# A four-layer decoder kernel: VectorE takes the layer-norm statistics ahead of two additions, and TensorE's first scores wait for the raw maxima

## The reference

```python
x = x + attention(layernorm(x))           # 16 heads of 8 channels
x = x + cross_attention(layernorm(x), ctx)
x = x + feed_forward(layernorm(x))        # experts, BitLinear, experts, attention with experts
```

## Time and profile before

| what | value |
|---|---|
| median of three runs | 4897.14 us |
| the profiled execution | 4900.09 us |
| its span | 4898.2 us |
| mean granted TensorE clock | 0.889 of full speed |
| busy: TensorE, its weight loads | 4007.7 us (82%), 2918.6 us (60%) |
| busy: VectorE, ScalarE, POOL | 3203.4 us (65%), 2059.5 us (42%), 2994.6 us (61%) |

### The profile page before, as it was taken

One profiled execution on the slowest core, in us unless ns is written; L12 is line 12 of the kernel. 1 busy time (PEld: TensorE's weight loads), 2 busy tenths in 40 slices (PEclk: granted clock), 3 DMA queues, 4 the chain that ended last, 5 costly groups with the idle time before them and its releaser, 6 DMA issues. The chain is left out here.

```text
span 4898.2 us, 215645 instructions
## 1 busy us (share of the span) xinstructions
PE 4007.7 (82%) x85067; PEld 2918.6 (60%) x85076; DVE 3203.4 (65%) x10848; ACT 2059.5 (42%) x5737; POOL 2994.6 (61%) x4949
## 2 busy tenths in 40 slices
PE   8999977254899978656999997559879998889988
PEld 6777754132566666523777774335547776667766
DVE  5875668422344688787556874753337878888866
ACT  4555545011344444365555554112225543336632
POOL 6766632276455699688556762038876777777710
PEclk9999988555899998755999997879998999999999
DMA  3000012433100022200000002113431000000000
GB/s 94 5 13 19 19 28 57 78 62 54 37 0 0 18 39 39 35 1 1 2 0 15 22 18 54 42 46 75 77 62 35 0 15 16 16 9 1 0 13 24
DMA packets 380509, 139.58 MB, mean 28 GB/s; under 512 B 216487, under 2 KB 373239, under 8 KB 380055
## 3 DMA queue, kind: packets, MB, share of 16 engines
q1 hardware_dynamic: 345430, 107.60, 9.3%
q0 software_dynamic: 34816, 28.34, 4.0%
HBM read 91.46 MB, written 43.85 MB: 28 GB/s over the span
## 5 line engine op out<-in xcount | busy, mean ns | idle before, releaser
L1051 DVE TENSOR_REDUCE rowmax<-ps 128x16 f32<-128x1024 f32 x512 | 626.3, 1223 | 488.0 <-PE ps L678 487.7
L696 PE MATMUL ps<-prob,kT 32*64 32x256 f32 x9216 | 781.7, 408 | 8.7 <-issue 2.4
L721 PE MATMUL ps<-v,probT 64*64 64x64 f32 x36864 | 764.6, 227 | 5.3 <-issue 2.2
L721 PEld LDWEIGHTS ps<-v,probT 64*64 64x64 f32 x36864 | 683.8, 140 | 57.4 <-issue 16.0
L678 PE MATMUL ps<-kblock,qT 32*64 32x256 f32 x8192 | 697.0, 410 | 17.2 <-DVE rowmax L1060 14.2
L900 ACT ACTIVATE probT<-ps 128x1024 f32<-128x1024 f32 x512 | 518.0, 1012 | 353.4 <-PE ps L708 353.0
L585 POOL TENSOR_TENSOR kblock<-kT,key_scale 128x512 f32<-128x512 f32 x576 | 599.8, 1041 | 18.2 <-ACT kT L878 7.6
L587 POOL TENSOR_TENSOR prob<-qT,key_scale 128x512 f32<-128x512 f32 x576 | 601.5, 1044 | 0.0
L561 POOL TENSOR_TENSOR vareps<-moments,eps 128x1 f32<-128x1 f32 x522 | 98.8, 189 | 745.7 <-DVE negmean L1025 745.6
L887 ACT ACTIVATE xn<-x_res,nmr,rstd 128x128 f32 (+1 forms) x512 | 252.7, 494 | 513.6 <-POOL nmr L567 349.5
L708 PEld LDWEIGHTS ps<-mT,pick_bf 32*64 32x64 bf16 x16384 | 311.7, 108 | 221.2 <-ACT mT L857 74.1
(11 more groups left out here) (380 smaller groups left out, 9655.7 us busy)
## 6 DMA issues: line engine op xcount, KB each, us to landing
ctxT<-in_ctxT SPq DMA_DIRECT2D x256, 64.0 KB, 1.8
held<-in_g_w SPq DMA_DIRECT2D x16, 836.0 KB
ctxT<-in_ctxT SPq DMA_DIRECT2D x256, 32.0 KB, 1.9
table<-prob SPq DMA_DIRECT2D x32, 256.0 KB, 2.4
x_dram<-x_res SPq DMA_DIRECT2D x32, 256.0 KB, 2.4
x_res<-x_dram SPq DMA_DIRECT2D x16, 512.0 KB, 6.9
x_res<-in_x SPq DMA_DIRECT2D x8, 512.0 KB, 7.5
x_res<-in_e_w SPq DMA_DIRECT2D x64, 64.0 KB
```

The lines of the kernel that those rows point to most:

```text
L696: mm = nc.tensor.matmul(out.rearrange("p (h s) -> p h s", h=GH), k.kT[rows, buf, S * b:S * b + S], k.qblock[rows, buf, :, S * b:S * b + S] ...
L721: mm = nc.tensor.matmul(k.ps_o[S * b:S * b + S, u, S * hh:S * hh + S], k.probT[rows, buf, at:at + S], k.v9[rows, buf, (HD + 1) * h:(HD + 1 ...
L1051: nc.vector.tensor_reduce(spread, heads, AX.X, ALU.max).then_inc(soft.did["max_raw"], 1)
```

## The change

In `scores_writable` TensorE waits for `max_raw` (L1051 has read the bank `s1`) in place of `max_done` (L1060 is through). In VectorE's step the output addition and the value bias move from ahead of the incoming tile's statistics to behind them. The four statistics instructions, their waits and the two additions are the same as before.

```diff
     def scores_writable(score1, score2, it):
         if score1 is not None:
-            after(pe, c, "max_done", it, 4)
+            after(pe, c, "max_raw", it, 4)
             after(pe, c, "kblock_done", it, 3)
...
             post_sums(post, pb, it, par)
-        if out is not None:
-            xt = stream_of(k, out.name)[:, out.columns()]
-            after(dve, c, "bias_done", it, 8)
-            dve.wait_ge(c.yv_psum, it - 2)
-            nc.vector.tensor_tensor(xt, xt, k.ps_y, ALU.add).then_inc(out.did["y_read"], 1)
-        if value is not None and value.name in VALUE_BIAS:
...
         early = c.prenormed(it, -PRENORM)
...
         if start is not None and not both:
...
             nc.vector.tensor_scalar(k.negmean[:, par, 0:1], k.meanvar[:, par, 0:1], -1.0, None,
                                     ALU.mult).then_inc(start.did["mv_done"], 1)
+        if out is not None:
+            xt = stream_of(k, out.name)[:, out.columns()]
+            after(dve, c, "bias_done", it, 8)
+            dve.wait_ge(c.yv_psum, it - 2)
+            nc.vector.tensor_tensor(xt, xt, k.ps_y, ALU.add).then_inc(out.did["y_read"], 1)
+        if value is not None and value.name in VALUE_BIAS:
...
         if guard is not None:
```

More of the change, by code:

```diff
@@ L1026, in step @@
                                     ALU.mult).then_inc(start.did["mv_done"], 1)
+        if out is not None:
[4 more added lines that the diff above has]
+        if value is not None and value.name in VALUE_BIAS:
+            bias = k.bv[:, value.a, :]
+            dve.wait_ge(c.yv_psum, it - 2)
+            if value.name == "L1_xattn":
+                after(dve, c, "v_done", it, 3 + NB)
+                nc.vector.tensor_tensor(k.v_sum[:, b3, :], k.ps_v, bias, ALU.add).then_inc(value.did["v_raw"], 1)
+            else:
+                after(dve, c, "o_psum", it, 3 + NB)
+                nc.vector.tensor_tensor(values(k, b3), heads_of(k.ps_v), heads_of(bias),
+                                        ALU.add).then_inc(value.did["v_done"], 1)
         if guard is not None:
```

## The result

The changed kernel takes **4981.45 us** (median of six runs, 4976.48 to 4994.65) against 4896.65 us before (six runs, 4893.37 to 4898.26): a ratio of 1.0177 with the 95% interval 1.0164 to 1.019, 85 us slower. The forecast was 4968, with 4912 to 4992 as its range. The total was right; two of its parts were not, and they cancelled.

What follows compares the result with a forecast made beforehand. Unmasked attention stages were taken as a ring of two arms meeting at POOL's kblock, masked ones as held by TensorE. Order +71 us, wait 0: 4900.1 + 71 = 4971, less 3 to the median, 4968 us; range 4912 to 4992.

Steps and rivals of the forecast that it cites:

- the longer arm: L0_attn, L2_xattn, L3_attn, L3_ffn: statistics arrive last at kblock, kT has 0.39 to 0.64 us slack; the move makes kT last.
- 0.53 behind L1019, plus 0.15 - 0.08 = 0.07, in all 0.60 us later: L0_attn: output addition L992 starts behind L1025, so oT and all later ScalarE instructions, kT included, come 0.60 us later.
- I take 0.09 us from ScalarE's or VectorE's end to the next engine's start: Handover between engines, read from L992's end to oT's start and also used from kT's end to POOL's kblock: 0.09 us.
- 0.30: L0_attn: later kT delays kblock, +0.30 us a step; the like terms were +0.19 in L2_xattn and +0.23 in L3_attn.
- +0.49 + 0.20 = +0.69: L3_ffn, us a step: kblock 0.49 later for kT, plus 0.20 because L1057 falls into L587 and L1060 follows.
- L3_xattn, -0.22: The one stage where the move pays: statistics no longer behind L1001, which stood 0.22 ahead of L1019; -0.22 us a step.
- The cover of L1001's own delay: L3_xattn: TensorE is idle before it needs oT, so L1001's delay costs nothing; without this cover up to 0.60 us.
- The masked stages' cover: L0_xattn, L1_attn, L2_attn: TensorE sets the step and needs the later kT and mT only later; costed at 0.
- Rival (c): Masked stages lose their cover and L585's delay counts in 180 steps: +34 to +54 us, 5002 to 5022; chance 0.08.
- I take 0, being nearest to the row that is not released by L1060: Masked stages, new wait ahead of L794: gain between 0 and 0.25 us a step, taken as 0.
- rival (a): The masked wait was real: L794 comes up to 0.25 us earlier, -45 us, total 4923; chance 0.18.
- the forecast's 1.19 a step: Sum of the order's terms over five stages, 0.30 + 0.19 + 0.23 + 0.69 - 0.22; times 60 steps, +71 us.

Runs made afterwards that it cites:

- e4: Changed kernel with ScalarE evicting qT and kT ahead of mT and xnT, TensorE waiting for mT and xnT by themselves: 4935.90 us.
- e9: Kernel before with max_raw wait, statistics first in L3_xattn, additions mid-statistics in L0_attn, L2_xattn, L3_attn and between L3_ffn's two sets: 4854.68 us.
- e5: Changed kernel with the waits of the two additions, not the additions, put ahead of the statistics: 4980.09 us.
- e6: Changed kernel with POOL waiting for s2_psum ahead of kT_done instead of behind it: 4977.42 us.
- e2: Kernel before with only VectorE's order changed, TensorE still waiting for max_done: 5033.61 us, ratio 1.0288.
- e1: Kernel before with only TensorE's wait changed to max_raw, VectorE's order as before: 4844.90 us, ratio 0.9899.
- e3: Changed kernel with the additions ahead of the statistics again in L3_ffn alone: 4930.50 us, ratio 1.0082.

## Why the total was right and its parts were not

- **Who is the longer arm, and that the move turns it over: right.** kblock is released by kT in all four stages named, and e4 and e9 show both sides of it: with kT earlier the step falls, and with a delay inside the slack it doesn't grow.
- **"0.53 behind L1019, plus 0.15 - 0.08 = 0.07, in all 0.60 us later": too small.** L1016 starts not 0.07 behind the start of the short L1010, but 0.19 in the step of L0_attn, 0.30 in that of L2_xattn, 0.21 in that of L3_attn and 0.13 in that of L3_ffn (0.21 in most). e5 brings it to 0.12 or 0.13 with the waits moved ahead, so most of it is the passing of waits. It can't be all: in L3_xattn L1025, with two waits ahead of it too, starts 0.08 behind L1010.
- **"I take 0.09 us from ScalarE's or VectorE's end to the next engine's start": wrong towards POOL,** 0.16 (0.14 in e6). In L0_attn 0.30 + 0.12 + 0.07 = 0.49, and 0.50 was measured. The terms of L2_xattn and L3_attn were short in the same way: 0.19 + 0.23 + 0.07 = 0.49 and 0.23 + 0.14 + 0.07 = 0.44, and the steps read have 0.50 and 0.43. The means are 0.40 and 0.53, since the steps of a loop's turn differ.
- **L3_ffn, "+0.49 + 0.20 = +0.69": mechanism right, first part mis-sized, and a term missing.** The 0.20 was measured as 0.19 and the 0.49 as 0.65. To it came 0.09 in most ordinary steps, from the waits ahead of L1016, and 0.62 more at each loop turn (0.02 before), which the sum did not have at all. The granted clock also fell, to 0.90 in 4400 to 4650, where it was 1.00 before. But it isn't the clock that lengthens the step: the ordinary steps that a stretch at the lower level touched take 5.78 or 5.79 us like those at the full level (two apart, 6.51 and 5.11), and the turns 6.41 like the others. In e9, at 1.00, the turn takes 0.57 more than the ordinary steps.
- **L3_xattn, -0.22: a third of it, -0.08.** "L1001 at 155.73 stood 0.22 ahead of L1019" was read rightly, but the 0.22 is not all won when L1001 goes: L1001 started 0.08 behind L927, and L1004 with its waits starts 0.21 behind it, so 0.13 is lost to the same passing of waits. e5, which puts more waits there, brings the whole gain down to nothing (6.14). The cover of L1001's own delay held.
- **The masked stages' cover:** it held in L1_attn and L2_attn (+0.02 each in e2), and gave way in L0_xattn (+0.14), about 7 us. Rival (c) was that in small.
- **"I take 0, being nearest to the row that is not released by L1060": wrong, and the largest error.** e1 puts the wait at -50 us; rival (a) had said -45. The gap that the profile calls "issue" was read as the time of passing eight waits. It shrank from 0.54 to 0.32 with the same number of waits, so it held the wait for L1060.
- **The sum.** The order was to cost 71 us and cost 139; the wait was to bring nothing and brought 50. Over the 48 middle steps the order is 48 x 2.64 = 127 us by the table, where the forecast's 1.19 a step gives 57. Errors of +68 and -50, and 4 us that the halves together give back, leave one of 14 us in a total that looks well predicted. The mechanism of the order was right and its size half of the true one; that the total fell so near is luck.

## What to carry to other kernels

Where two arms meet, write down the slack of the arm that you delay in every stage, subtract the handover to that very engine (mostly 0.16 us to POOL here, 0.09 to ScalarE), and delay it by less: in L0_attn 0.20 us made the step shorter, 0.72 made it 0.50 longer. Read more than one step of a loop turn: the step at the turn, and in L3_attn one more, moved by other amounts than the ordinary one. A part that goes by in a sum at nothing deserves its own run, since a total can be right by two errors. And when a wait moves from the last to an earlier instruction of a chain, don't trust a gap labelled "issue" to be the price of issuing: compare it with the time of the event that was awaited.

## What the runs showed of the hardware

- A small VectorE instruction that begins beside POOL's 128x512 product ends with it: 0.17 us became 0.68 to 1.04, and which of two such instructions is caught decides 0.2 us of the step (944 and 315 ns before, 175 and 809 after, in L3_ffn). With POOL's addition moved away the last one takes 0.17 again. The Trainium skill ("SBUF — State Buffer", section "SBUF: two separate sides") has this as an exclusive lock for a whole instruction, between a VectorE operation with two SBUF inputs and a GpSimd operation that reads SBUF, and the rows agree.
- VectorE starts an instruction 0.08 us before the end of the one ahead when that one is 0.28 us long, even with two waits between (L1025 behind L1016 in L3_attn). Behind the negative mean of 0.15 us the addition with its two waits starts between 0.02 before and 0.16 after its end, and 0.03 before it with the waits moved ahead (e5). L1025 in L3_xattn, 0.07 before that end with two waits, doesn't fit; the cause stays open.
- In L3_ffn TensorE's wait for mT grew to 1.28 us in the step shown, and the mean granted clock over steps 12 to 60 was 0.90 of 2.4 GHz after the change and in e2, with stretches at 1.2 GHz among those at 2.4; it was 1.00 before, in e3 and in e9. So longer idle stretches of TensorE went with a lower clock. The steps were hardly longer for it: 5.78 or 5.79 us with such a stretch, 5.79 without.
- The turn of the loop costs VectorE 0.53 us in L3_ffn behind an L1060 of 0.17 us, and nothing that shows behind one of 0.96 us (before the change and in e3).
